# Routing weights transposed in 32x32 blocks on VectorE, and stored in four pieces

## The reference

```python
x = x + attn(layernorm(x), wq, wk, wv, wo)      # linear attention, D = 64
x = x + ffn(layernorm(x), Wr, bias, Wg, Wu, Wd, conv_w, conv_b)
# ffn:
scores = sigmoid(x @ Wr)                        # 8 experts
_, idx = top_k(scores + bias, 2)
w = take_along_axis(scores, idx); w = w / (sum(w) + 1e-9)
cw = zeros((T, 8)).at[arange(T), idx].add(w)    # weight of each expert per token
routed = sum over e < 4 of cw[:, e] * (silu(x @ Wg[e]) * (x @ Wu[e])) @ Wd[e]
routed += (cw[:, 4] + cw[:, 6]) * x + cw[:, 7] * relu(x)
out = routed + causal depthwise conv of 4 taps over tokens
```

## Time and profile before

| | |
|---|---|
| median of 3 runs | 885.39 us (885.03 to 885.51) |
| the profiled execution | 888.19 us, its span 886.4 us |
| granted TensorE clock, mean | 0.988 |
| busy: TensorE / VectorE / ScalarE / GpSimd | 96% / 85% / 73% / 46% |
| chain that ended last | TensorE 77%, VectorE 12%, ScalarE 4% |

### The profile page before, as it was taken

The page is one execution under the profiler, slowest core; times in us unless marked ns, Lnnn a source line. Parts: engine busy times, 40 slices in busy tenths (PEclk is TensorE's granted clock), DMA queues, the critical chain, the costliest instruction groups (busy, mean ns, idle before and its releaser), DMA issues.

```text
span 886.4 us, 16852 instructions
## 1 busy us (share of the span) xinstructions
PE 852.9 (96%) x5437; PEld 757.1 (85%) x5437; DVE 751.2 (85%) x2093; ACT 643.2 (73%) x1366; POOL 409.6 (46%) x585
## 2 busy tenths in 40 slices
PE   5878999999999999999999999999999999899997
PEld 4667888999889988889899998889988998788886
DVE  4668889988899988999899998999889988678884
ACT  4585867787777777787678777777867875666653
POOL 3214635554455454455355544545535544433332
PEclk9899999999999999999999999999999999999999
DMA  9112354433354442434443344554424344324434
GB/s 286 60 43 54 119 144 138 112 110 100 116 143 143 143 120 67 126 125 138 143 121 104 100 132 120 143 144 126 111 75 131 109 121 119 96 54 118 118 94 119
DMA packets 79447, 103.86 MB, mean 117 GB/s; under 512 B 6528, under 2 KB 58880, under 8 KB 79360
## 3 DMA queue, kind: packets, MB, share of 16 engines
q1 hardware_dynamic: 74752, 86.02, 30.6%
q0 software_dynamic: 4608, 16.78, 10.0%
HBM read 68.96 MB, written 17.04 MB: 97 GB/s over the span
## 4 chain that ended last, share of the span: by engine, by line
PE 77%; DVE 12%; ACT 4%; issue 3%; POOL 2%; DMA 1%; POOLq 0%; DVEq 0%; ACTq 0%
PE ps_gu L410 11%; PE ps_gu L412 10%; PE ps_gu L411 10%; PE ps_sh L541 6%; PE ps_y L410 6%; PE ps_y L411 6%; PE ps_y L412 6%; PE ps_y L460 3%; PE ps_sh L531 3%; PE ps_sh L484 2%; ACT x L842 2%; PE ps_sh L588 1%; PE ps_sh L589 1%; PE ps_gram L618 1%; PE ps_gu L564 1%
## 5 line engine op out<-in xcount | busy, mean ns | idle before, releaser
L1391 POOL TENSOR_TENSOR gate<-gate,cwb 128x512 f32<-128x512 f32 x128 | 168.0, 1313 | 291.4 <-ACT gate L765 265.6
L410 PE MATMUL ps_gu<-x2T_hi,wgu_hi 128*128 128x512 f32 x512 | 211.3, 413 | 1.2 <-DVE hid L1055 1.2
L412 PE MATMUL ps_gu<-x2T_hi,wgu_lo 128*128 128x512 f32 x512 | 202.2, 395 | 0.0
L411 PE MATMUL ps_gu<-x2T_lo,wgu_hi 128*128 128x512 f32 x512 | 201.7, 394 | 0.0
L410 PE MATMUL ps_y<-wd_hi,hid_hi 128*128 128x256 f32 x512 | 153.1, 299 | 2.2 <-DVE hid_lo L1062 2.2
L1073 DVE SCALAR_TENSOR_TENSOR conv<-x2T,conv_w,conv 128x512 f32<-128x512 f32 x192 | 150.6, 822 | 0.0
L411 PE MATMUL ps_y<-wd_lo,hid_hi 128*128 128x256 f32 x512 | 145.4, 284 | 0.0
L412 PE MATMUL ps_y<-wd_hi,hid_lo 128*128 128x256 f32 x512 | 145.0, 283 | 0.0
L1062 DVE TENSOR_TENSOR hid_lo<-hid,hid_hi 128x512 fp32r<-128x512 f32 x101 | 86.2, 853 | 46.2 <-ACT hid_hi L758 46.2
L412 PEld LDWEIGHTS ps_gu<-x2T_hi,wgu_lo 128*128 128x128 f32 x512 | 96.6, 189 | 22.2
L410 PEld LDWEIGHTS ps_gu<-x2T_hi,wgu_hi 128*128 128x128 f32 x512 | 97.2, 190 | 18.4 <-issue 2.3
(11 more groups left out here) (126 smaller groups left out, 1877.5 us busy)
## 6 DMA issues: line engine op xcount, KB each, us to landing
cwb<-cw_rows SPq DMA_DIRECT2D x128, 256.0 KB, 4.0
xa<-in_x SPq DMA_DIRECT2D x32, 512.0 KB, 7.8
acc<-in_x SPq DMA_DIRECT2D x32, 512.0 KB, 6.9
acc<-x POOLq DMA_DIRECT2D x32, 512.0 KB, 4.6
out<-acc SPq DMA_DIRECT2D x64, 256.0 KB, 2.6
cwb<-in_wg SPq DMA_DIRECT2D x4, 128.0 KB, 3.9
cwb<-in_wu SPq DMA_DIRECT2D x4, 128.0 KB, 3.7
cwb<-in_wd SPq DMA_DIRECT2D x1, 512.0 KB, 4.5
```

The source lines that it names most:

```text
L410: nc.tensor.matmul(dst, a_hi, b_hi, start=start, stop=False, skip_group_check=True)
L411: nc.tensor.matmul(dst, a_hi, b_lo, start=False, stop=False, skip_group_check=True)
L412: return nc.tensor.matmul(dst, a_lo, b_hi, start=False, stop=stop, skip_group_check=True)
L1391: g.tensor_tensor(gate[:, e % 2], gate[:, e % 2], cwb[:, q, e], ALU.mult).then_inc(gatew_ready, 1)
```

## The change

TensorE's transposition, ScalarE's copy and their semaphore `cwT_done` are removed. VectorE transposes the whole 128x32 tile `cw` in blocks of 32x32 right behind the instruction that makes it, into a tile `cwT` of 128x32: partitions 32j to 32j+15 then hold the 16 wanted rows for the tokens 32j to 32j+31. SP stores them with four DMAs of 16x32 in place of one of 16x128, and waits for all four. `xn_transpose` of half 1 and `x2_transpose` of half 1 no longer wait for `cwT_ready`.

```diff
-        cwT = sb("cwT", [EM * TG, P])
+        SQ = 32
+        assert NE * TG == SQ
+        cwT = sb("cwT", [P, SQ])
...
                 sp.wait_ge(cwT_ready, st.before("R", 1, 1))
-                sp.dma_start(rows.rearrange("a e (t n) -> (a e t) n", t=TG), cwT[:, :]).then_inc(cw_stored, 16)
-                sp.wait_ge(cw_stored, st.before("R", 16, 16))
+                for j in range(P // SQ):
+                    sp.dma_start(rows[:, :, :].rearrange("a e (t n) -> (a e t) n", t=TG)[:, j * SQ:(j + 1) * SQ],
+                                 cwT[j * SQ:j * SQ + EM * TG, :]).then_inc(cw_stored, 16)
+                sp.wait_ge(cw_stored, st.before("R", 64, 64))
...
-                if c == 1 and st.on("R"):
-                    pe.wait_ge(cwT_ready, st.before("R", 1, 1))
-                elif st.on("B"):
+                if st.on("B"):
                     pe.wait_ge(x1_ready, st.before("B", 2, 2 - c))
...
-                elif c == 0:
+                else:
                     pe.wait_ge(x1_ready, st.before("B", 2))
-                else:
-                    pe.wait_ge(cwT_ready, st.before("R"))
...
-            def weights_transpose(st):
-                pe.wait_ge(cw_ready, st.before("R", 1, 1))
...
-                nc.tensor.transpose(ps_sh[1][0:EM * TG, 0:P],
-                                    cw[:, st.slot("R", 2), 0:EM].rearrange("p e t -> p (e t)"), ident[:, :])\
-                    .then_inc(cwT_done, 1)
...
-                if drain:
-                    down(st, "C", 2)
-                if r_on:
-                    weights_transpose(st)
                 if a_on and r_on:
                     xn_transpose(st, 0)
-                if c_on and not drain:
+                if c_on:
                     down(st, "C", 2)
...
-            def weights_copy(st):
-                act.wait_ge(cwT_done, st.before("R", 1, 1))
...
-                copy(cwT[:, :], ps_sh[1][0:EM * TG, 0:P]).then_inc(cwT_ready, 1)
...
-                    dve.wait_ge(cwT_done, st.before("R", 1, -1))
                 v.tensor_tensor(cw[:, q].rearrange("p e t -> p t e"), raw[:, :, 0:NE],
                                 winv[:, :].unsqueeze(2).broadcast_to([P, TG, NE]), ALU.mult).then_inc(cw_ready, 1)
                 assert issued[0] == RT
+                dve.wait_ge(cw_ready, st.before("R", 1, 1))
+                if st.later("R", 1):
+                    dve.wait_ge(cw_stored, st.before("R", 64))
+                v.transpose(cwT[:, :], cw[:, q].rearrange("p e t -> p (e t)")).then_inc(cwT_ready, 1)
```

More of the change, by code:

```diff
@@ L285, in program @@
         cw_ready = sem("cw_ready")
-        cwT_done = sem("cwT_done")
         cwT_ready = sem("cwT_ready")
@@ L402, in _ @@
                 sp.wait_ge(out_stored[k], 32 * (NG // 4))
-            sp.wait_ge(cw_stored, 16 * NG)
+            sp.wait_ge(cw_stored, 64 * NG)
         @block.tensor
@@ L591, in attention @@
                 last.then_inc(attn_done, 1)
-            def weights_transpose(st):
-                pe.wait_ge(cw_ready, st.before("R", 1, 1))
-                if st.on("B"):
-                    pe.wait_ge(x1_ready, st.before("B", 2, 1))
-                else:
-                    pe.wait_ge(x2Tlo_ready, st.before("R", HC, HC))
-                nc.tensor.transpose(ps_sh[1][0:EM * TG, 0:P],
-                                    cw[:, st.slot("R", 2), 0:EM].rearrange("p e t -> p (e t)"), ident[:, :])\
-                    .then_inc(cwT_done, 1)
             def chain_gramT(st):
@@ L679, in head @@
                 gate_up(at("C", 0, NG), 1)
-                weights_transpose(r)
                 q_project(at("Q", 4, NG))
@@ L909, in conv_begin @@
                         .then_inc(tap_ready, 1)
-            def weights_copy(st):
-                act.wait_ge(cwT_done, st.before("R", 1, 1))
-                if st.later("R", 1):
-                    act.wait_ge(cw_stored, st.before("R", 16))
-                copy(cwT[:, :], ps_sh[1][0:EM * TG, 0:P]).then_inc(cwT_ready, 1)
             def xnT_head(n, c):
@@ L960, in head @@
                 conv_begin(r)
-                weights_copy(r)
                 q_high(at("Q", 4, NG))
@@ L1019, in body @@
                     norm1(st)
-                if r_on:
-                    weights_copy(st)
                 if st.on("B") and st.drain():
```

## The result

| | before | changed |
|---|---|---|
| median | 885.21 us (884.3 to 885.51, 4 runs) | **889.67 us** (888.32 to 891.27, 4 runs) |
| ratio | | **1.0053** (95% interval 1.0033 to 1.0072) |
| profiled execution, its span | 888.19 us, 886.4 us | 888.32 us, 886.5 us |
| period of four steps (group 10's `cw` to group 14's) | 104.11 us | 104.58 us |
| group 0's `cw`, group 26's `cw` | 59.55, 734.97 us | 59.73, 738.51 us |

The changed kernel is slower by 0.53%, 4.5 us with an interval of 2.9 to 6.4 us. The two spans shown look alike only because the profiled execution of before was granted TensorE's half clock (1.2 GHz) from 771.4 to 778.2 us, just ahead of the drain, and that of the changed kernel wasn't. So the comparison goes by steps at full clock.

A forecast was written before the change was run, and what follows sets the result against it. In the middle TensorE's list was taken as the time, other work costing only where that list waits. Head and middle +1.8, drain -2.8, last group +0.3 gave -0.7 us: 884.7 us, called no change, range 882.0 to 888.6.

The forecast's parts named there:

- What VectorE gets: On VectorE behind `cw`: a transposition of 0.22 us, starting 0.24 us after `cw`, moves everything behind it by 0.24 us.
- TensorE's part: In the middle: removing TensorE's transposition gains 0.11 us in each of 20 ordinary steps where nothing else is late.
- Where d lands in the middle: Path to norm 2's fourth slice: chain steps lose 0.24 us each; ordinary steps change by +0.11, -0.04 or -0.07 us.
- d: The delay of all VectorE work behind the added transposition: 0.24 us, with bounds of 0.12 and 0.46.
- Head and middle: From the start through the middle groups: a net gain of 1.8 us, written +1.8.
- ScalarE in the middle: In the middle: ScalarE's freed time buys nothing, since norm 2 starts with its factors.
- The drain: Groups 28 to 30: two TensorE waits of 0.47 us per step vanish, 3 x -0.94, so -2.8 us.
- SP: Stores and `cwb` loads on SP: nothing in the middle, loads 0.6 us later but covered in drain, +0.3 last group.
- rival 3: Stores landing 3.5 us after issue delay the loads, costing drain steps and last group: 888.1 us; chance 0.07.
- The sum: Whole kernel: +1.8 - 2.8 + 0.3 = -0.7 us, giving a median of 884.7 us, called no change.
- rival 2: VectorE becomes the bound: with d = 0.42 chain and other steps wait longer, +4.3 us, 889.7 us; chance 0.15.

The follow-up runs named there:

- e11: The changed kernel with GpSimd weighting only 256 of the 512 columns of the fourth expert's gate; 881.39 us, ratio 0.9943.
- e12: The kernel before with GpSimd weighting only 256 of the 512 columns of the fourth expert's gate; 881.55 us, ratio 0.9938.
- e2: The kernel before with a VectorE transposition of `cw` added into an unused tile, TensorE's transposition, ScalarE's copy and the one store kept; 890.43 us, ratio 1.0067.
- e3: The changed kernel without any transposition, its four stores taking a constant tile as soon as `cw` is ready; 881.94 us, ratio 0.9959.
- e7: The changed kernel with four buffers of `x2` instead of two; 887.46 us, ratio 1.0014.
- e5: The changed kernel with VectorE's transposition moved behind the statistics of norm 2, except in drain steps; 898.86 us, ratio 1.0148.
- e1: The changed kernel with one store of 16x128 from a constant tile instead of four, VectorE's transposition kept; 888.07 us, ratio 1.0034.
- e10: The kernel before with four buffers of `x2` instead of two and nothing else; 885.57 us, ratio 0.9992.
- e4: The changed kernel with a second VectorE transposition of `cw` behind the first, into an unused tile; 891.94 us, ratio 1.0078.
- e6: The changed kernel with VectorE's transposition one place later, behind `hid_lo` of expert 2, except in drain steps; 885.49 us, ratio 0.9998.

## Why the prediction was wrong

The forecast was 884.7 us in a range of 882.0 to 888.6, and the change measures 889.67 us. Point by point:

- **What VectorE gets**: right. The transposition starts 0.25 to 0.26 us after `cw` (0.24 forecast), takes 0.211 us (0.22), and all behind it moves by 0.24 us (0.24).
- **TensorE's part**, "its removal is worth 0.11 us in each of the 20 ordinary steps ... in which nothing else is late": the size is about right (0.10 to 0.13 us in e11 against e12), but in the changed kernel something else was late in every step. e2, which keeps TensorE's work, has the same period. Without the addition the removal gives 0.50 us per period (e3).
- **Where d lands in the middle**: this step failed. It followed the path from the statistics to norm 2's fourth slice with `cw` itself held fixed against TensorE, and asked only how much slack stood there. The place was right, as TensorE does wait for that slice; but `cw` isn't fixed. It is the end of the round, and in an ordinary step the round took as long as TensorE's list (24.97 us, against 24.96 on average in e12). A delay that the slack hides in one step is still there at the next `cw`, and comes on top in the next. The sign was in the trace of before, in `raw`: 0.5 to 0.95 us in the middle against 0.19 us in group 0, each time ending with GpSimd's gate. I had read the earlier trace rows as "anything else costs only where it makes that list wait", and the list of waits holds only semaphores. Ordinary steps were to change by +0.11, -0.04 and -0.07 us; they changed by +0.24, +0.24 and +0.14. Chain steps were to lose 0.24 and got 0.15 us shorter (29.09 to 28.94). TensorE's wait for the fourth slice was to be 0.68 us in chain steps and up to 0.22 in the step behind; it is 0.35 and 0.27 to 0.29 in every ordinary step. The period was forecast at 104.3 us, measured 104.58. Head and middle came to +3.5 us (group 26's `cw`, 734.97 to 738.51) instead of +1.8, of which 3.1 lie between the `cw` of groups 2 and 26.
- **ScalarE in the middle**: "norm 2 starts with its factors" was read from the chain step alone. In groups 12, 13 and 14 of the kernel before it started 0.34, 0.50 and 0.53 us after the last factor had started, in the changed kernel 0.24. The sum used 0.23 throughout, so this moved nothing in it.
- **The drain**: this step failed too, and for another reason. "Both waits go: 3 x -0.94" counted norm 2 done by 838.9, since its factors were there. It overlooked the wait on the accumulating DMA, which landed, by its 4.6 us, only some 0.6 us ahead of the end of the wait that went. The three steps gained 0.06, 0.51 and 0.54 us, 1.1 instead of 2.8. With that DMA off the path they gain 1.2 to 1.3 each (e7).
- **SP**: the stores leave 0.49 us after `cw` (0.46 forecast), and in the drain the loads leave 3.23 us after it, where it was 2.26: 1.0 later instead of 0.6. In the last group they leave 0.2 us earlier, not 0.3 later. In the middle their cover held, as forecast (GpSimd waits for `cwb` 8 times in both kernels), though behind chain steps' `cw` the loads leave 0.6 us later (4.87 us against 4.23 in group 11); e5 shows how far the cover reaches. The median landing of 3.1 us came close to rival 3's condition (3.5), but it cost nothing in the middle, where the stores now leave 3 us earlier. In the drain, where rival 3 had its price, they landed in 1.4 us. The Trainium skill, "DMA: Bandwidth & Descriptors" (Specifications), made the stores' 128 B rows suspect. In e1 a single store with 512 B rows, issued at the same place, landed no sooner, so no run here shows a price of the short rows.
- **The sum**: by steps of the two profiled executions it is +3.5 for head and middle, -1.1 for the drain and -0.1 behind group 31's `cw`, together +2.3 us. The step from group 27 to 28 can't be compared with before, where the clock was halved. Against e10, where it wasn't, it adds 0.2 (29.07 against 28.86). The medians differ by 4.5 us. The lower end of the interval, 2.9 us, is close to the 2.5 accounted for; where the rest lies, if it is there, the traces don't tell. The heads of the profiled executions scatter by more than that: from group 0's `cw` to group 1's it takes 23.84 to 28.17 us in the 14 traces.
- **The rivals**: rival 2 gives 889.7 us, but by d = 0.42 and norm-2 waits of 0.22 to 0.40 us, and d was 0.24. Its number fits and its mechanism doesn't. The case that occurred, a round outside TensorE that was already as long as TensorE's list in ordinary steps, stood in none of the rivals.

## What to carry to other kernels

An engine that is busy 99.9% of a period isn't therefore the only bound. Before you cost an addition elsewhere at its slack, follow one value of the addition's engine from step to step until it comes back to itself. If that round has the length of the step, nothing absorbs an addition on it: it comes back in every step (here 0.97 us per period against e3), and once the round sets the pace, a removal on the busy engine gives nothing back (e2 against the changed kernel). By itself the removal was worth 0.50 us per period here, so try both changes alone and together. Look in the round for instructions that last longer than their own kind does elsewhere: they hide waits that no list of waits shows. And when a removed wait was long, write down the second latest condition of the same instruction, DMAs with it. An instruction that must read its neighbour's result was cheaper one place later.

## What the runs showed of the hardware

- A 32-column `raw` on VectorE took 0.19 to 1.2 us, by how long GpSimd's 512-column multiplication beside it went on; where it was held, it ended 0.05 us after it (e11: 0.19 in the median, with a gate of 0.74 us instead of 1.30). A `conv` tap of 512 columns (0.74 us) that started during GpSimd's `hid_lo` ended 0.55 us after it. The time counts as VectorE's busy time.
- A transposition of 128x32 fp32 on VectorE in blocks of 32x32 takes 0.21 us (0.17 as the second in e4). Its place in the list costs 0.24 us right behind its input, 0.13 us one instruction later (e6), and 0.09 us where it waits for nothing (e4).
- The accumulating DMA from GpSimd lands 4.5 to 5.2 us after its issue, for 512 KB added; as a condition for reusing a buffer it outlasts most of what stands around it in a drain step.
- A small store that mostly landed in 1.4 us in the kernel before took 3.1 us in the median over the run when issued right behind `cw`, and 3.7 us with a single store in place of four (e1). At that time the accumulating DMA, issued 0.6 us before `cw`, is under way; in the drain, where it was issued 4.5 us before `cw`, the stores took 1.4 us. That this is the reason was not tried.
